# Third and last stage together: where a block's four gate products stand, when the pair sums come, and decays behind the gates

## What is computed

```python
xn = layernorm(x); xs, z = split(xn @ W_in); xs = silu(causal_conv(xs))   # c
dt = softplus(xs @ dt_w + dt_b); B = xs @ B_w; C = xs @ C_w
h = h * exp(dt * A) + (dt * xs)[..., None] * B;  y = sum(h * C) + xs * D
out = x + (y * silu(z)) @ W_out
h = silu(lin(x, w1)) * lin(x, w2)                                          # d
h = gelu(lin(h, h1)); h = gelu(lin(h, h2)); out = lin(h, w3)
```

## Time and profile before

| what | value |
|---|---|
| median of 3 executions | 1022.95 us (1021.24 to 1026.63) |
| the profiled execution | 1027.38 us |
| its span, first to last instruction | 1025.6 us |
| busy: PE, weight loads, DVE, ACT, POOL | 858.2, 694.7, 681.8, 573.3, 446.5 us |
| mean granted clock of TensorE | 0.864 of full |
| stages c and d | from some 501 us to the end |
| chain that ended last | PE 65%, DVE 17%, ACT 8%, issue 5% |

### The profile page before, as it was taken

One profiled execution on the slowest core, in us unless ns is written; L12 is line 12 of the kernel. 1 busy time (PEld: TensorE's weight loads), 2 busy tenths in 40 slices (PEclk: granted clock), 3 DMA queues, 4 the chain that ended last, 5 costly groups with the idle time before them and its releaser, 6 DMA issues.

```text
span 1025.6 us, 21514 instructions
## 1 busy us (share of the span) xinstructions
PE 858.2 (84%) x8256; PEld 694.7 (68%) x8256; DVE 681.8 (66%) x1997; ACT 573.3 (56%) x1072; POOL 446.5 (44%) x771
## 2 busy tenths in 40 slices
PE   4888845789999999897678669999798988887995
PEld 4777735668888888776546457778576766766774
DVE  4877864757888887652487768676876858673431
ACT  3444532346666666556467467565858667444541
POOL 1755762314555554434367544335353524341000
PEclk9766865559999999887687779999999999999898
DMA  8300002000000000000000000000000000000000
GB/s 274 100 13 17 24 22 64 22 1 2 2 2 2 2 3 2 1 2 1 1 0 1 1 0 2 1 0 12 1 11 1 12 1 6 6 11 0 11 1 20
DMA packets 22149, 16.76 MB, mean 16 GB/s; under 512 B 2576, under 2 KB 20376, under 8 KB 21792
## 3 DMA queue, kind: packets, MB, share of 16 engines
q1 hardware_dynamic: 21040, 14.77, 4.7%
q10 hardware_dynamic: 1008, 0.63, 0.2%
HBM read 11.20 MB, written 4.19 MB: 15 GB/s over the span
## 4 chain that ended last, share of the span: by engine, by line
PE 65%; DVE 17%; ACT 8%; issue 5%; POOL 3%; DMA 1%; ACTq 0%; POOLq 0%; SPq 0%; DVEq 0%
PE ps L1580 12%; PE ps L1582 9%; PE ps L1581 9%; PE ps L1659 6%; PE ps L1593 6%; PE ps L1881 3%; PE ps L1999 3%; PE ps L1652 2%; PE ps L1575 2%; PE ps L1599 2%; PE ps L1935 1%; DVE vbd L1047 1%; PE ps L1941 1%; PE ps L1683 1%; DVE a_ln_st L108 1%
## 5 line engine op out<-in xcount | busy, mean ns | idle before, releaser
L1580 PE MATMUL ps<-h_h,wh_h 128*128 128x512 f32 x256 | 106.4, 416 | 10.6 <-DVE h_l L1429 6.5
L1582 PE MATMUL ps<-h_l,wh_h 128*128 128x512 f32 x256 | 101.7, 397 | 0.0
L1581 PE MATMUL ps<-h_h,wh_l 128*128 128x512 f32 x256 | 101.5, 396 | 0.0
L1659 PE MATMUL ps<-w_e,he 128*128 128x128 f32 x512 | 87.0, 310 | 3.7 <-ACT he L719 3.3
L719 ACT ACTIVATE he<-ps,pp 128x256 f32<-128x256 f32 x128 | 59.6, 471 | 43.5 <-PE ps L1582 39.0
L1659 PEld LDWEIGHTS ps<-w_e,he 128*128 128x128 f32 x512 | 76.9, 221 | 6.1 <-ACT he L719 5.4
L1593 PEld LDWEIGHTS ps<-mov,hbd 32*128 32x128 f32 x2048 | 78.5, 233 | 0.0
L1593 PE MATMUL ps<-mov,hbd 32*128 32x32 f32 (+1 forms) x2048 | 77.4, 308 | 0.0
L577 POOL TENSOR_TENSOR term<-term 128x224 f32<-128x224 f32 (+2 forms) x48 | 38.9, 811 | 84.2 <-DVE term L1316 81.7
L1580 PEld LDWEIGHTS ps<-h_h,wh_h 128*128 128x128 f32 x256 | 49.2, 192 | 27.0 <-DVE h_l L1429 9.0
L117 POOL TENSOR_TENSOR b_ln_ve<-b_ln_mv,eps 128x2 f32<-128x2 f32 x64 | 13.1, 204 | 110.9 <-DVE b_ln_mv L111 110.9
(11 more groups left out here) (292 smaller groups left out, 2581.6 us busy)
## 6 DMA issues: line engine op xcount, KB each, us to landing
x<-in_x SPq DMA_DIRECT2D x16, 128.0 KB
w_h<-in_w_h SPq DMA_DIRECT2D x2, 1024.0 KB, 8.3
x<-x SPq DMA_DIRECT2D x16, 128.0 KB, 1.8
xB<-x SPq DMA_DIRECT2D x32, 64.0 KB
out_x<-xB SPq DMA_DIRECT2D x32, 64.0 KB
w_m<-in_w_m SPq DMA_DIRECT2D x3, 256.0 KB, 5.8
xB<-in_w_e SPq DMA_DIRECT2D x1, 512.0 KB
w_e<-in_w_e SPq DMA_DIRECT2D x1, 512.0 KB
```

The source lines that it names most:

```text
L1580: pe.matmul(dst, a_h, b_h, start=start, stop=True, skip_group_check=True)
L1581: pe.matmul(dst, a_l, b_h, start=False, stop=True, skip_group_check=True)
L1582: return pe.matmul(dst, a_h, b_l, start=False, stop=True, skip_group_check=True)
L1659: last = pe.matmul(ps[:, ACC, P * c:P * c + P], he[e % 2][:, P * c:P * c + P], w_e2[:, e, :], start=False, stop=True, skip_group_check=True)
```

## The change

- In steps 0 to 3 (`WHOLE`) all four head groups of `pairs(n+1)` are multiplied at the end of step n into banks 4 to 7, which no block uses yet, and `terms` runs once over all of them. On VectorE `add_sums`, `summed_steps` and `statistics(n+4)` move forward there, `inputs_by_chunk` back.
- In an even step TensorE does gate products 0, 1 and 2 of the entering block, with the halves of the ending block's last product between them. Product 3 comes in the odd step, in front of `from_states`. The first two hidden products stand in front of `pairs(n, 1)`; in even steps `hidden(1, 1)` does too.
- ScalarE makes `decays(n)` of an odd step only in that step, behind `gated(3)`, `high0(2)` and `high0(3)`. `in_and_out` moves from the end of the even step to behind `high0(1)`. `silus` and `normed` come in front of `hidden1`, `output_norm` between its halves, `states_out` behind it.
- VectorE makes `raised(1)`, `conv_input(n+3)` and `low0(0)` in the even step, and `raised(2)`, `raised(3)` and all `low0` early in the odd step, in front of `decay_products`.
- `high0(b, 0)` of blocks 1 to 5 waits for the whole last product of the block before.
- Step 16 becomes `last_step`: block 6's four gate products come in it, and banks are given out so that they don't wait for each other's `raw`; the last product of block 5 comes behind them, from `hid_behind`. VectorE's `last_step` has `tokens_in(6)`, `from_states`, `add_sums`, `gated` of sequence 15, then `low1(5, 2)` and `low1(5, 3)`, then block 6. ScalarE's has `hidden2` of block 5, then `gated` and `high0` of block 6, then `output_norm(14)`. The tail loses what has moved.

The core of the diff ("..." marks what is left out):

```diff
@@ -344,6 +344,7 @@
         he_ps, he_ready, e_done = (sem(n) for n in ("he_ps", "he_ready", "e_done"))
...
         NDB = 2 * NB // 4
+        WHOLE = 4
         LAST = NDB - 1
...
@@ -908,6 +908,9 @@
                 if b == 0 and m == 0:
...
                     act.wait_ge(m_low, 2 + HID)
+                if m == 0 and 1 <= b < LAST - 1:
+                    act.wait_ge(S["d_y_ps"], b)
                 act.wait_ge(m_raw, nth(b, m))
...
@@ -929,74 +932,89 @@
                 entering, middle, ending = block_of(n, 4), block_of(n, 5), block_of(n, 6)
...
                     in_and_out(1)
+                if middle is not None:
+                    high0(middle, 1)
+                    if have(1):
+                        in_and_out(n + 1)
                 if have(1):
...
                     transposed_input(n + 2)
+                if middle is not None:
+                    gated(middle, 3)
+                    high0(middle, 2)
+                    high0(middle, 3)
+                    if have(0):
+                        decays(n)
                 if have(1):
...
                     skip_path(n)
-                if middle is not None:
-                    high0(middle, 1)
-                    gated(middle, 2)
-                if ending is not None:
-                    hidden2(ending, 0)
-                if have(2):
+                if have(2) and middle is None:
                     normed(n + 2)
                 if ending is not None:
-                    hidden2(ending, 1)
-                if middle is None and have(0):
+                    for m in range(HID):
+                        hidden2(ending, m)
+                        if m == 1 and have(0):
+                            chunk_weights(n)
+                elif middle is None and have(0):
                     chunk_weights(n)
-                if ending is not None:
-                    hidden2(ending, 2)
-                    hidden2(ending, 3)
                 if entering is not None:
...
                 if middle is not None:
-                    high0(middle, 2)
-                    gated(middle, 3)
+                    if have(2):
+                        normed(n + 2)
+                    hidden1(middle, 0)
+                    hidden1(middle, 1)
                     if have(0):
                         chunk_weights(n)
-                    high0(middle, 3)
+                    if have(-2):
+                        output_norm(n - 2)
+                    hidden1(middle, 2)
+                    hidden1(middle, 3)
+                    if have(0):
+                        states_out(n)
+                if entering is None and have(1):
+                    decays(n + 1)
                 if entering is not None:
                     gated(entering, 0)
-                    if have(-2):
-                        output_norm(n - 2)
-                    if have(0):
-                        states_out(n)
+                if middle is None and have(-2):
+                    output_norm(n - 2)
+                if middle is None and have(0):
+                    states_out(n)
+                if entering is not None:
                     gated(entering, 1)
-                if have(1):
-                    decays(n + 1)
-                if entering is not None:
                     high0(entering, 0)
-                if middle is not None:
-                    hidden1(middle, 0)
-                if entering is None and have(-2):
-                    output_norm(n - 2)
-                if middle is not None:
-                    hidden1(middle, 1)
-                if entering is None and have(0):
-                    states_out(n)
-                if middle is not None:
-                    hidden1(middle, 2)
-                    hidden1(middle, 3)
-                if have(2):
+                    gated(entering, 2)
+                if entering is None and have(2):
                     in_and_out(n + 2)
...
@@ -1307,16 +1326,22 @@
                     if t + 1 < NB:
...
                         dve.wait_ge(S["c_bcT"], t + 2)
-                dve.wait_ge(S["c_g1_ps"], 2 * t + k + 1)
+                if t < WHOLE:
+                    lo, hi, count = 0, 4, 2
+                    dve.wait_ge(S["c_g1_ps"], 2 * t + 2)
+                else:
+                    lo, hi, count = 2 * k, 2 * k + 2, 1
+                    dve.wait_ge(S["c_g1_ps"], 2 * t + k + 1)
                 w = wall[l][:, :, :, :].rearrange("p c s t -> p s c t")
-                split = lambda v: v.rearrange("p s (g c) t -> p s g c t", g=4)[:, :, 2 * k:2 * k + 2]
+                split = lambda v: v.rearrange("p s (g c) t -> p s g c t", g=4)[:, :, lo:hi]
+                banks = ps[:, PAIRS:PAIRS + hi - lo, :]
                 dve.tensor_tensor(split(term[l][:, 0:HALF * PAIR].rearrange("p (s c t) -> p s c t", s=HALF, t=CH)),
                                   split(w[:, HALF:CH]),
-                                  ps[:, PAIRS:PAIRS + 2, 0:WIDE].rearrange("p g (s c t) -> p s g c t", s=HALF, t=CH), ALU.mult)
+                                  banks[:, :, 0:WIDE].rearrange("p g (s c t) -> p s g c t", s=HALF, t=CH), ALU.mult)
                 dve.tensor_tensor(split(term[l][:, HALF * PAIR:].rearrange("p (s c t) -> p s c t", s=HALF, t=HALF)),
                                   split(w[:, 0:HALF, :, HALF:CH]),
-                                  ps[:, PAIRS:PAIRS + 2, WIDE:BC_AT].rearrange("p g (s c t) -> p s g c t", s=HALF, t=HALF),
-                                  ALU.mult).then_inc(S["c_term"], 1)
+                                  banks[:, :, WIDE:BC_AT].rearrange("p g (s c t) -> p s g c t", s=HALF, t=HALF),
+                                  ALU.mult).then_inc(S["c_term"], count)
...
@@ -1452,82 +1477,109 @@
                 entering, middle, ending, leaving = (block_of(n, k) for k in (4, 5, 6, 7))
...
                     tokens_in(entering)
-                if have(2):
+                if have(2) and middle is None:
                     conv_input(n + 2)
+                if middle is not None:
+                    raised(middle, 2)
+                    low0(middle, 1)
                 if leaving is not None:
                     tokens_out(leaving)
-                if middle is not None:
-                    raised(middle, 1)
                 if ending is not None:
...
                     low1(ending, 3)
+                if middle is not None:
+                    from_states(n - 1)
+                    raised(middle, 3)
+                    low0(middle, 2)
+                    low0(middle, 3)
                 if have(0):
                     decay_products(n)
-                if have(-1):
+                if middle is None and have(-1):
                     from_states(n - 1)
-                if middle is not None:
-                    low0(middle, 0)
-                    low0(middle, 1)
-                    raised(middle, 2)
                 if have(0):
                     terms(n, 0)
+                if n < WHOLE and have(-1):
+                    add_sums(n - 1)
                 if have(1):
...
                     outputs_by_chunk(n + 1)
-                if middle is not None:
-                    low0(middle, 2)
-                    if have(1):
-                        summed_steps(n + 1)
-                    raised(middle, 3)
-                if have(0):
+                if middle is not None and have(1):
+                    summed_steps(n + 1)
+                if n >= WHOLE and have(0):
                     terms(n, 1)
-                if middle is not None:
-                    low0(middle, 3)
-                elif have(1):
+                if n >= WHOLE and middle is None and have(1):
                     summed_steps(n + 1)
                 if have(-1):
-                    add_sums(n - 1)
+                    if n >= WHOLE:
+                        add_sums(n - 1)
                     gated(n - 1)
+                if n < WHOLE:
+                    summed_steps(n + 1)
+                    statistics(n + 4)
                 if have(1):
...
                     carried(n)
-                if have(1):
+                if n >= WHOLE and have(1):
                     inputs_by_chunk(n + 1)
...
                     states(n)
+                if n < WHOLE:
+                    inputs_by_chunk(n + 1)
                 if entering is not None:
                     tokens_low(entering)
-                if have(4):
+                if n >= WHOLE and have(4):
                     statistics(n + 4)
...
                     c_ln2.stats(dve, chain, lambda b: c_r[(n - 1) % 4][:, b, :], (n - 1) % 4)
+                if entering is not None:
+                    raised(entering, 1)
+                    if have(3):
+                        conv_input(n + 3)
...
@@ -1924,16 +1977,16 @@
                 l = t % 2
...
                     pe.wait_ge(S["c_prod"], t + 1)
-                if t == 0 and k == 0:
+                if t == 0:
...
                     pe.wait_ge(S["c_term"], 2 * t + k)
```

(73 more changed lines are left out.)

104 lines of the change are left out of this document (72 added, 32 removed).

## The result

The changed kernel is slower: 1043.58 us (median of 4, 1040.75 to 1045.45) against 1024.79 for the kernel before in the same comparison, ratio 1.0172 with a 95% interval of 1.0109 to 1.0234. The forecast of 1015.0 and its range (to 1024) missed it. The profiled execution took 1045.45 us, with a span of 1043.7.

A forecast was written before the change was run, and what follows sets the result against it. VectorE was taken to pace steps 0 to 3; later, TensorE even steps, with waits in odd ones. Terms -8.2 -2.8 +2.5 +1.6 -3.1 -1.6 -1.5 +5.1 gave -8.0, from the median 1022.95 to 1015.0 us; range 1000 to 1024.

The forecast's parts named there:

- The end: After the steady steps: waits laid out as 14 us for 15.5 before, -1.5, bounds -9 and +3.
- the last wait of step 14: Step 14: a TensorE wait of 1.6 us goes because a hidden product now stands before the pairs, -1.6.
- Block 0: Steps 4 and 5: no block in front covers the gates, 3.3 us more then 0.8 less, +2.5.
- The term of step 4: Step 4: `tokens_in(0)` waits 3.1 us for POOL's `stored(1)`; earlier statistics leave 0.3, gain 2.8, bounds 0 and 3.1.
- The clock: TensorE behind 4.2 us waits before steps 6, 8, 10, 12: half clock, 1.7 us at three, +5.1, bounds 0 and 13.6.
- the layout of an odd step: Odd step: decays at 8.2 us, even step's transpose at 29.75, with a new 4.2 us wait for POOL's store.
- pairs +0.5 each: Steps 6 to 11: 0.97 us less against 1.5 more in the even step; three pairs lose 0.5 each, +1.6.
- A: Steps 0 to 3: early whole pair products remove VectorE's waits of 6.7 and 1.5 us, gain 8.2, bounds 4 and 9.
- D: Steps 12 and 13: without later statistics TensorE bounds step 13, 25 us for 29.7, less 1.5 in step 12, -3.1.
- The rivals: Chances: no transpose wait or clock up 0.28, half the start's gain missing 0.22, late decays 0.14, doubled table switches 0.02.
- decays late: ScalarE, odd steps: decays beyond 1.15 us slack; slower from 2.7 us late, 1031 at 3.5; chance 0.14.
- The table switch at double price: ScalarE loses a second 1.28 us per load, delaying the third hidden product 5.1 us in four pairs: 1035.5; chance 0.02.

The follow-up runs named there:

- before_whole: The kernel before with only the whole chunk products of steps 0 to 3 and VectorE's order there: 1015.13 us, 0.9911 of the kernel before.
- the split: Changed kernel with the ten low parts of the MLP's last weights dealt over steps 0 to 3 instead of 0 to 4: 1037.80 us.
- the filler: Changed kernel with 15 unread matmuls on TensorE in front of the transposes of steps 6, 8, 10 and 12: 1027.81 us.
- the end (14.0): Changed kernel with only the last step and the tail rearranged on ScalarE, VectorE and GpSimd: 1028.49 us.
- the fastest version: Changed kernel with the store, split and end edits plus three more moves in each block's two steps: 988.10 us, 0.9624 of the kernel before.
- halves_behind: The 988.1 us kernel with the last product whole behind the third gate product, not in halves between gate products: 1011.59 us.
- store_first: Changed kernel with GpSimd's skips and store of step n-2 in front of the scales of step n+4: 1024.69 us.

## Why the prediction was wrong

By its own steps, from the largest miss (stretches as in the table):

- **The end** (E): forecast -3.1 with the last wait of step 14, measured +6.8. The list of waits had the right members but one (in step 14, below). 1.75, 2.6 and 0.8 us came as 1.56, 2.56 and 0.80. But the states were put at 1.5 and took 4.33, because ScalarE's third Gelu waits 7.95 us for `low1(5, 0)` at the end of VectorE's step, and the states come out behind it. Step 14 lost its old wait of 1.6 us but got a new one of 1.29 for the states (878.33), with a spell of 3.4 us behind it; the transpose of block 5's tokens starts 19.9 us after the step's start, where it was 18.9 before and 17.3 by the forecast. Block 7's tokens were put at 4.2 and took 5.97. And the clock's loss was priced only before the steps 6 to 12, though the text counted pauses as long as these in the end.
- **Block 0** (B): forecast -0.3, measured +7.5. The term of step 4 was right (2.8 forecast; B is 3.4 shorter in the start's part alone). The failed step is the one missing from the text: of an instruction that is moved forward, the waits it carries must be read. `low0(0, 0)` has one for the ten low parts, 6.5 us on TensorE, a term that the prediction put at nothing without naming it.
- **The clock** (C and D): the mechanism was right and the size off. I took the short spell of 3.41 us at three of four pauses, 1.7 each, 5.1. It was the long one, 6.8 us, at all four, 2.2 to 2.8 us each, and 1.4 us came with the pause of 1.78 in step 7, which was not priced: 9.0 in C, and 2.6 in D (57.5 against 54.9 filled), 11.6. My upper bound (13.6) held it; the earlier trace rows had both spells, and I chose the row of 4.29 us for its length. The row of 2.35 us with its 6.83 us spell should have warned me. That trace also has spells of 3.4 us behind pauses of 3.39 us (608.25) and 2.17 us (997.63), which the prediction doesn't count.
- **Right:** the layout of an odd step. Decays 8.2 us after its start (735.78 less 727.59), the third hidden product's wait 1.78 for 1.7, odd step's start to the transpose 29.85 for 29.75, the transpose's wait 4.07 for 4.2 in the four places named and none before step 14, gate products 3.22 us apart, pairs +0.5 each with no spell in either kernel, +1.6 for the three as forecast. Steps 1 to 3 take 15.4 to 15.8 us for 15; A gave 6.7 of 8.2. D without its clock loss gave 1.9 of 3.1.
- **The rivals:** none was the case. The one that ends slower (decays late) is excluded, since `pairs` waits 0.7 us once in the whole of both stages. It carried the long spell's price, but tied to a condition that was not needed. The table switch at double price did not show: at 733.54 a load of 1.28 us starts, the exponential at 734.84.

The 28.5 us that stand against the start's 10 lie, by stretches against `before_whole`, in B (11.0), C (9.8), D (0.6) and E (6.5). Each of them has an edit that takes it back: in B the split (5.9) and the store (6.2), in C the store (9.6) or the filler (9.0), in E the end (14.0). The edits' gains overlap and don't add up to a ledger. Whether the kernel before would reach 988 us with the start's part and the same repairs was not tried, so what the new order of gates and decays is worth against the old one stays open.

## What to carry to other kernels

When a step is moved forward, list the semaphores its instructions carry, each with the time that it is met now. A wait that is free at the old place can be the longest at the new one. Price a pause of TensorE as the pause plus what runs slowly behind it: here 4.1 plus 2.2 to 2.8 us. And before a layout is judged by its time, look for the one late transfer in it: here moving two GpSimd calls in front of six tiny operations was worth 19 us in the changed kernel, and 5 in the kernel before.

## What was not expected of the hardware

- Idle TensorE cost more than busy TensorE. Fifteen useless matmuls (3.78 us) in each of four pauses made the kernel 15.8 us faster between medians (13.4 in the stretches of one execution each).
- Short pauses are not all alike. In the fastest version, with 1.10 us and less (and one of 1.56 at 871.0), no spell at 0.50 came from 597 to 875 us, and with `halves_behind`'s 1.56 none from 595 to 891; a pause of 1.78 in the filled kernel was followed by one of 3.4 us in 2 of 5 places (at 615.6 and 851.1), in the changed kernel in 3 of 5. But in `store_first` the pauses of 1.17 to 1.28 us at the transposes had a spell of 3.4 us behind them in 4 of 4. So the length of the pause alone doesn't tell; what else does stays open. Pauses of 4.05 to 4.08 us brought 6.8 us each time, in 16 of 16 places in four kernels.
- The stage's start moved by up to 10.6 us (493.45 to 504.08) between executions with the same work ahead of it, so one profile's span can't tell a change of 1%.
